# Software pipelining of a transformer layer over 16 sequences: output product and first normalisation of a sequence placed in the next sequence's attention half, its feed-forward one half later

## The reference, cut to what matters

```python
x = _layernorm(x + attention(x))        # 16 heads of 16, window of 128 keys; 4 latent heads; sigmoid gate mixes
x = _layernorm(x + ffn(x))              # ternary weights, 256 -> 1024 -> 256, exact gelu, RMS norm ahead of each
# attention: mixed = gate * local + (1 - gate) * remote;  return mixed @ out_w + out_b
# ffn:       h = gelu(rms(x) @ w_up_q.T);  return rms(h) @ w_down_q.T
```

## Time and profile before

| what | value |
|---|---|
| median of 3 runs | 1309.5 us (1309.12 to 1319.59) |
| profiled execution, its own time | 1306.51 us |
| its span, first to last instruction | 1304.8 us |
| busy: PE, DVE, ACT, POOL | 1071.0, 963.8, 666.2, 686.1 us |
| mean granted clock of TensorE | 0.922 of full speed |
| first exponential of body 0, body 14, body 15 | 120.5, 1161.7, 1229.5 us |

### The profile page before, as it was taken

How to read it: one execution, slowest core, us unless ns; L and a number is a source line. 1 busy time by engine, 2 the same in 40 slices (tenths; PEclk the granted TensorE clock), 3 DMA queues, 4 the chain that set the end, 5 groups by cost and what they waited for, 6 DMA issues and landing times.

```text
span 1304.8 us, 37906 instructions
## 1 busy us (share of the span) xinstructions
PE 1071.0 (82%) x15776; PEld 685.5 (53%) x15776; DVE 963.8 (74%) x2048; ACT 666.2 (51%) x1026; POOL 686.1 (53%) x870
## 2 busy tenths in 40 slices
PE   2566889798988989897998989899888989795855
PEld 1344555464655556464655556465555646464533
DVE  5856768778787887878787877878787887866445
ACT  1213555564646556464646556364655556462624
POOL 6542637373654736364554637265473737364553
PEclk9778989899998999899999989899998989997887
DMA  5845180735537181644628082543719173541000
GB/s 153 139 79 110 43 139 30 125 64 91 92 75 123 37 134 48 115 82 76 107 66 132 30 136 54 106 76 76 122 44 137 46 120 69 98 68 35 2 18 17
DMA packets 57019, 108.08 MB, mean 83 GB/s; under 512 B 14192, under 2 KB 40944, under 8 KB 53744
## 3 DMA queue, kind: packets, MB, share of 16 engines
q1 hardware_dynamic: 56848, 105.66, 44.1%
HBM read 71.55 MB, written 34.08 MB: 81 GB/s over the span
## 4 chain that ended last, share of the span: by engine, by line
PE 52%; DVE 28%; ACT 9%; issue 4%; POOL 4%; SPq 1%; DMA 1%; DVEq 0%; POOLq 0%; ACTq 0%
PE work L1477 9%; PE oacc L1405 7%; PE oacc L1424 6%; PE work L1230 5%; PE work L1348 5%; PE scores L1385 3%; DVE x L1058 3%; PE work L1415 3%; ACT Pt L760 3%; DVE x L1066 3%; DVE nmax L1000 2%; PE scores L1230 2%; DVE ytok L1134 2%; DVE Pt L966 2%; DVE lat_st L963 2%
## 5 line engine op out<-in xcount | busy, mean ns | idle before, releaser
L760 ACT ACTIVATE Pt<-scores 128x1024 f32<-128x1024 f32 (+1 forms) x256 | 228.3, 914 | 115.4 <-PE oacc L1405 83.2
L626 POOL TENSOR_TENSOR h_lo<-hbuf,h_hi 128x512 f16<-128x512 f32 x128 | 148.3, 1159 | 249.6 <-DVE h_hi L1114 249.6
L1000 DVE TENSOR_REDUCE nmax<-work 128x3 f32<-128x480 f32 x352 | 216.5, 636 | 27.8 <-PE work L1353 23.9
L598 POOL TENSOR_SCALAR_AFFINE_SELECT Pt<-Pt 128x512 f32<-128x512 f32 x256 | 163.2, 638 | 109.6 <-ACT Pt L760 108.1
L1477 PE MATMUL work<-xnT,wup_t 128*128 128x512 f16 x512 | 156.6, 444 | 32.5 <-DVE xnT L1102 32.1
L1348 PE MATMUL work<-Ks,Qs 98*32 98x160 bf16 x4096 | 141.5, 237 | 33.0 <-DVE nmax L1000 28.7
L1405 PE MATMUL oacc<-Pt,Vp 128*32 128x256 f32 (+1 forms) x2048 | 149.6, 359 | 3.5 <-POOL Pt L602 3.0
L1255 PE MATMUL scores<-xT,wqk 128*128 128x512 f32 x256 | 116.5, 609 | 19.3 <-ACT xT L695 19.3
L1385 PE MATMUL scores<-Qs,Ks 100*32 100x160 bf16 (+4 forms) x4096 | 113.7, 228 | 13.5 <-ACT Pt L760 10.1
L602 POOL TENSOR_SCALAR_AFFINE_SELECT Pt<-Pt 128x512 f32<-128x512 f32 x192 | 122.0, 635 | 0.0
L1424 PE MATMUL oacc<-wdn_t,h_hi 128*128 128x256 f16 x512 | 120.2, 276 | 0.2
(11 more groups left out here) (169 smaller groups left out, 2088.8 us busy)
## 6 DMA issues: line engine op xcount, KB each, us to landing
parts_scratch<-parts SPq DMA_DIRECT2D x96, 256.0 KB, 6.8
Qs<-parts_scratch SPq DMA_DIRECT2D x96, 256.0 KB, 9.2
Ks<-parts_scratch SPq DMA_DIRECT2D x96, 256.0 KB, 8.9
xtok<-L_attn_x SPq DMA_DIRECT2D x16, 512.0 KB, 13.7
xres<-L_attn_x SPq DMA_DIRECT2D x16, 512.0 KB, 14.8
y<-ytok SPq DMA_DIRECT2D x16, 512.0 KB, 3.2
Qs<-L_ffn_w_up SPq DMA_DIRECT2D x1, 1024.0 KB, 5.6
Qs<-L_ffn_w_down SPq DMA_DIRECT2D x1, 1024.0 KB, 7.6
```

Source lines behind the costliest of these rows:

```text
L598: ins = pool.affine_select(out=pt[:, :, 0:P], in_=pt[:, :, 0:P], compare_op=ALU.is_gt, fill=0.0, base=0, pattern=[[0, 4], [1, P]], channel ...
L626: pool.tensor_tensor(h_lo[:, t % NR, :], hbuf[:, t % 2, :], h_hi[:, t % NR, :], ALU.subtract).then_inc(h_lo_ready, 1)
L760: nc.scalar.activation(Pt[:, u % NPT, :, 0:w], scores[:, slot, :, :].rearrange("p k (h q) -> p (k h) q", h=2)[:, :, 0:w], ACT.Exp, scale=S ...
L1000: nc.vector.tensor_reduce(nmax[:, :, :].rearrange("p b h -> p (b h)")[:, first:first + n], work[:, slot, 0:n * BAND].rearrange("p (h c) -> ...
```

## The change

The change makes a body carry three sequences. The attention half of s now also holds the "early" steps of sequence s-1: transpose of the mix, output product, statistics, normalisation, transpose and split in two float16 parts, spread over the units by a table. The second half holds the feed-forward of s-1, the gate of s (three steps "G") and the projections of s+2. There are 17 bodies; the first has no s-1, the last has only s-1.

Work changes engines: `h_hi` is a second gelu on ACT in place of DVE's cast; the sum of the mix, the product `lat_bd` and the low part of the normalised x go from DVE to POOL (the last by way of a new float32 copy `xnF` that ACT makes). The third and second parts of query and key slices get steps of their own ("R"). The statistics of the last normalisation come at the end of the second half ("L"), its scaling in units 2 to 5 of the body after. `mixed`, `xnF` and a second `ytok` are new buffers.

```diff
+EARLY = {1: [MIX_T], 2: [MIX_T + 1], 4: [OUT], 5: [OUT + 1], 6: [STATS], 8: [NORM], 9: [NORM_X],
+         12: [XN_T], 13: [XN_T + 1], 14: [XN_HI], 15: [XN_HI + 1, XN_LOW], 16: [XN_LOW + 1]}
 SECOND_HALF = (
-    ("P", X_T), ("F", GATE), ("P", QK), ("F", MIX), ("P", QK + 1), ("P", QK + 2), ("P", QK + 3),
-    ("F", MIX_T), ("P", LAT_IN), ("F", OUT), ("P", VALUES), ("P", VALUES + 1), ("P", LAT_SCORES),
-    ("F", NORM), ("P", LAT_SCORES + 1), ("P", VALUES + 2), ("P", VALUES + 3), ("F", XN_T),
-    ("P", LAT_NORM), ("F", UP), ("F", UP + 1), ("P", LAT_T), ("F", UP + 2), ("P", LAT_T + 1),
-    ("F", UP + 3), ("P", LAT_O), ("F", UP + 4), ("P", REMOTE), ("F", UP + 5), ("P", REMOTE + 1),
-    ("F", UP + 6), ("F", UP + 7), ("F", END))
+    ("P", X_T), ("G", GATE_O), ("P", QK), ("F", UP), ("R", 0), ("P", QK + 1), ("F", UP + 1), ("R", 1),
+    ("P", LAT_IN), ("P", QK + 2), ("F", UP + 2), ("R", 2), ("P", QK + 3), ("F", UP + 3), ("R", 3),
+    ("G", GATE_Z), ("P", LAT_SCORES), ("P", LAT_SCORES + 1), ("P", VALUES), ("F", UP + 4), ("G", GATE_MIX),
+    ("P", VALUES + 1), ("F", UP + 5), ("P", VALUES + 2), ("F", UP + 6), ("P", VALUES + 3),
+    ("P", LAT_NORM), ("F", UP + 7), ("P", LAT_T), ("P", LAT_T + 1), ("F", END), ("P", LAT_O),
+    ("P", REMOTE), ("P", REMOTE + 1), ("L", 0))
+def attention_step(u):
+    order = [("S", u + 1)] if u + 1 < NU else []
+    order += [("A", v) for v in A_OF[u][:1]]
+    order += [("E", k) for k in EARLY.get(u, [])]
+    order += [("V", u - 2)] if u >= 2 else []
+    order += [("A", v) for v in A_OF[u][1:]]
+    order += [("O", (u - 7) // NB)] if u >= 7 and (u - 7) % NB == 0 and (u - 7) // NB < HG - 1 else []
+    return order + [("T", t) for t in range(2) if u == T_AT[t]]
...
-            def f_step(s, k):
-                if k == GATE:
+            def gate_step(s, k):
+                if k == GATE_MIX:
 
                     pool.wait_ge(gate_g, count(s, 1, 0))
                     for b in range(NB):
                         rv = rem[:, s.par, b, 0:D].rearrange("p (h d) -> p h d", h=H)
                         pool.tensor_tensor(rv, rv, gate[:, 2, b, :].unsqueeze(2).to_broadcast([P, H, HD]),
                                            ALU.mult).then_inc(rem_part, 1)
+                        pool.wait_ge(rem_part, count(s, NB, b))
+                        pool.wait_ge(mixed_part, count(s, NB, b))
+                        pool.tensor_tensor(mixed[:, b, :], mixed[:, b, :], rem[:, s.par, b, 0:D], ALU.add
+                                           ).then_inc(mixed_ready, 1)
...
-                    gelu = nc.scalar.activation(hbuf[:, t % 2, :], work[:, slot, :], ACT.Gelu)
+                    nc.scalar.activation(hbuf[:, t % 2, :], work[:, slot, :], ACT.Gelu).then_inc(h_act, 1)
+                    if t >= NR:
+                        act.wait_ge(down_done, count(s, FT, t - NR))
+                    nc.scalar.activation(h_hi[:, t % NR, :], work[:, slot, :], ACT.Gelu).then_inc(h_hi_ready, 1)
```

More of the change, by code:

```diff
@@ L164, in work_use @@
 def work_use(s, phase, k):
[L169 to L177, removed]
+    return WORK_USE[phase, s.i, k]
 def p_use(s, result):
-    at = (P_ORDER_FIRST if s.known and s.i < 2 else P_ORDER).index(result)
+    at = (P_ORDER_FIRST if s.i < 2 else P_ORDER).index(result)
     return at % 4, s.i * P_PER[at % 4] + at // 4
@@ L196, in over_sequences @@
 def over_sequences(body):
-    for i in range(B):
-        body(Seq(i, i % 2, i // 2))
+    for i in range(B + 1):
+        body(Seq(i))
 def build(nc, x, qkv_w, qkv_b, rq_w, rq_b, rkv_w, rkv_b, rout_w, rout_b, out_w, out_b, gl_w, gr_w,
@@ L329, in build @@
         oT_ready = sem("oT_ready")
+        g_vec = sem("g_vec")
+        xn_low = sem("xn_low")
         f_vec = sem("f_vec")
@@ L488, in body @@
                     load_x(later)
[L489 to L492, removed]
+                if s.i >= 2:
+                    store(Seq(s.i - 2))
+                if s.exists:
+                    load_xres(s)
+                if s.next().exists:
                     move_max(s.next())
@@ L755, in weights @@
                     act.wait_ge(pv_done, count(s, NU, u - NPT))
-                if u == 1 and not s.last:
+                if u == 1 and s.next().exists:
                     act.wait_ge(part2, count(s.next(), 4, 3))
@@ L811, in body @@
                         copy_o(s, (u - 6) // NB)
-                    if not s.last:
+                    if s.next().exists:
                         for t in range(2):
@@ L1160, in body, with last_norm @@
+            def last_norm(s, b):
+                if b == 0:
+                    dve.wait_ge(rstd2_ready, count(s, 1, 0))
+                y = ytok2[:, s.par, b, :]
+                nc.vector.tensor_scalar(y, y, mv[:, b, 0:1], rs[:, 0, b:b + 1], ALU.subtract, ALU.mult
+                                        ).then_inc(y_ready, 1)
             def body(s):
+                f, later = s.before(), s.second_next()
                 for u in range(FIRST_HALF):
-                    if u >= STAT_AT and not s.first:
-                        finish_before(s, u - STAT_AT)
@@ L1164, in body @@
[L1164 to L1177 removed]
+                    if 0 <= u - LAST_AT < NB and s.i >= 2:
+                        last_norm(Seq(s.i - 2), u - LAST_AT)
@@ L1372, in scores_T @@
                 slot, k = score_use(s, u)
-                if u < 2 and not s.last:
+                if u < 2 and s.next().exists:
                     for bank in (2 * slot, 2 * slot + 1):
```

549 lines of the change are left out of this document (291 added, 258 removed).

## The result

The changed kernel takes 1486.2 us (median of four runs, 1482.7 to 1486.8) against 1309.3 us for the kernel before: 1.135 times as long, interval 1.128 to 1.142. The direction was forecast, the size was not: 1372 us were predicted, with 1412 as the high end. The profiled execution spans 1484.8 us, 114.5 more than the predicted span.

A forecast was written before the change was run, and what follows sets the result against it. PE was to bound the first half, the DMA chain to the key copies to floor the second: 32.4 + 46.6 = 79.0 us per body. 120.5 + 66.3 + 13 x 79.0 + 156.5 = 1370, with 1.7 around it 1372; range 1314 to 1412.

The forecast's parts named there:

- 120.5 + 66.3 + 13 x 79.0 + 156.5 = 1370.3: Whole span: 120.5 us ahead of body 0, 66.3 for body 0, thirteen bodies of 79.0, 156.5 for bodies 14 to 16.
- First half: 26.6 + 5.8: First half of a body: 26.6 us of PE work plus 5.8 of waiting in order between engines, 32.4 together.
- The third rival: Second half: POOL and ACT pass the DMA floor, clock falls another 0.03 (1.5 us); body 83.4, total 1429; chance 0.11.
- the fourth rival: ACT stands as long again after each table load, 1.3 us on the path once per body: 1389; chance 0.05.
- Third part at 12.3: Second half: POOL finishes the third part of the second query slice at 12.3 us (11.5 to 13.5).
- Transfers from there to the landing, 34.0: Second half: DMAs from the end of that third part to the landed key copies take 34.0 us, unchanged.
- Second half 46.6: Second half of a body: 46.6 us (46.4 to 50), first maxima at 46.5, DMA floor 46.3.
- Slices 5 to 7 behind the gate on POOL: Second half: POOL's gate runs to 35.3 us; h_lo of slices 5 to 7 follows at 36.4, 38.4 and 40.3.
- Body 16: Last body: early steps alone 17, eight slices 19.5, end 3.9, last normalisation and store 8; 48.5 us.
- Body 14: Body without projections or DMA chain: first half 32 and second half 25, 57 us together.
- body 15: Body without maxima, projections or DMA chain: first half 26 and second half 25, 51 us together.
- Slower by over 1%: Whole kernel against the one before: the outcome slower had chance 0.82, faster by over 1% 0.06, within 1% 0.12.

The follow-up runs named there:

- x5: Changed kernel with 26 small filling products of PE per body, in unused columns beside the transposed maxima, ahead of maxima group 15: 1432.9 us (1.097).
- x6: x5 with four more groups of filling products, ahead of the first scores and in the second half of the changed kernel: 1410.8 us (1.080).
- x9: Changed kernel with the four sums of the gated mix given back from POOL to VectorE: 1509.6 us (1.157).

## Why the prediction was off

By its own sum, 120.5 + 66.3 + 13 x 79.0 + 156.5 = 1370.3. The trace after has 128.4, 65.8, 1105.7 and 184.9 in those places, so the 114.5 us are +7.9, -0.5, +78.7 and +28.4.

**Bodies 1 to 13, +78.7: the step that failed.** "First half: 26.6 + 5.8" priced PE's work at full clock because the old first half had 1.00, and left it there after adding 5.8 us of waits. The waits came to the sum priced (5.3 measured); the work took 32.5. x5 and x6 show that it is the clock: with fills in the waits and at 1.00 the bodies take 79.6, and 71.4 of the 78.7 us are back. The third rival had the mechanism, but in the second half and for 1.5 us; the second half's clock did fall as it said, from 0.93 to 0.89, but it was the first half that fell far, from 1.00 to 0.82.

The Trainium skill (ScalarE: Activation LUTs, What ACT_TABLE_LOAD costs) adds a drain of about 1380 ns to each load. That was the ground of the fourth rival, and the prediction said that no run could show it. The trace of before could, where the wait for PE behind a load is shorter than such a drain; in the trace of after ACT waits for nobody in this place. Before, then after:

```profile
1138.19 1.28 ACT L796 ACT_TABLE_LOAD   x1
1139.64 0.60 ACT L796 ACTIVATE hbuf<-work 128x512 f32<-128x512 f32 x1 [0.17 <-PE work L1477]
```
```profile
763.20 1.28 ACT L854 ACT_TABLE_LOAD   x1
764.49 0.60 ACT L854 ACTIVATE hbuf<-work 128x512 f32<-128x512 f32 x1
```

The GELU after starts 1.29 us after the load began, 1.28 of them the load itself, and the load begins 0.02 us after the ACTIVATE ahead of it has ended. Before, the GELU came 1.45 us after the load began, 0.17 of them a wait for PE. The measurement decides: 1.28 per load here, and that rival should have had no chance.

**The rest of the body held.** Third part at 12.3: 11.6. Transfers from there to the landing, 34.0: the key copies landed at 44.9 to 47.3 in bodies 1 to 13, so 33.3 to 35.7 us later, 33.9 in the median. Second half 46.6: 47.4. Slices 5 to 7 behind the gate on POOL, h_lo at 36.4, 38.4 and 40.3: the burst ran from 768.63 to 774.60 and the low parts ended at 775.75, 778.53 and 780.33, so at 35.3, 38.0 and 39.8.

**The end, +28.4.** Body 16 was right (48.5; 48.8). Body 14 was put at 57 and took 68.1, body 15 at 51 and took 68.0. Of these 28.1 us, 4.7 are the first half of body 14 (36.7 against 32), the same clock: in x6 it takes 32.5 at 1.00. The first half of body 15 (35.8 against 26) holds 12.1 us of idle time where the 26 left some 4 (old work 16.2 and 5.9 of early steps): without maxima to give between the scores PE waits 5.3 us for an exponential that stands behind ACT's normalised copy (1391.71 to 1393.33), itself late because DVE waited 2.78 us for the root on POOL before it made x1. The two second halves (31.4 and 32.2 against 25) have PE busy 20.5 and 22.1 at 0.89 and 0.81. How their 13.6 us divide between waits and clock, no run settles: no fills stood there.

**Prologue, +7.9: a move that I priced at nothing.** `lat_bd` went from DVE to POOL, and in the first sequence it stands there behind the reduction over partitions of the weight scale. After, POOL and PE:

```profile
47.52 0.40 POOL L664 PARTITION_ALL_REDUCE alpha<-alpha  x1 [8.29 <-issue]
55.36 0.71 POOL L603 TENSOR_TENSOR lat_bd<-rk_sb,diag_mask 128x256 f32<-128x256 f32 x1 [7.44 <-issue]
```
```profile
56.17 2.08 PE L1360 MATMUL scores<-lat_bd,rqT 64*128 64x256 f32 x8 [12.38 <-POOL lat_bd L603]
```

Before, DVE had made it at 43.01, and PE began at 43.95. The 7.44 us in which POOL waits for nothing that the profile shows are not new: before, the first TENSOR_TENSOR on POOL after the same reduction had 7.29 of it, at 81.44, and memsets stood between, the first of them 0.05 us behind the reduction. What POOL does in that time stays open. The move puts a step that PE needs into that place. All experiments on the changed kernel keep this cost. It was read from the trace and not tried by itself.

**The chances.** Slower by over 1% had 0.82, and the range ended at 1412. It had no case in which two halves lose clock together with a late prologue and a late end; the rivals were priced one at a time, and the three large errors had one sign.

## What to carry to other kernels

When steps are moved beside other work, price the work at the clock of a stretch that already has such waits, not at the clock of the stretch that it moves into; where only the clear stretch is at hand, keep the slow price as the range's end. A dependent wait of 3 us in the middle of PE's work cost twice: itself and the slower products behind it. Before sharing an engine's work out, look what stands behind each step in the new engine's queue, in the prologue and the last bodies too, and whether the relieved engine was on the path at all: here its casts weren't.

## What I had not expected of the hardware

In body 7's first half the granted clock fell to 1.2 GHz for 6.9 us at a time, with waits of PE of only 1.8 and 3.2 us ahead, and 26 small products put into the longer one kept it at 2.4 GHz there: 53 us over the whole run, at no cost in the wait. The first TENSOR_TENSOR on GpSimd after a reduction over partitions started 7.3 to 7.4 us late, in both kernels. Fills that had to wait themselves cost 5.5 us a body and gave nothing back. And four sums of 128x256 float32 took 4.29 us on VectorE while GpSimd worked beside it (x9, body 8) and 3.03 on GpSimd, though in the kernel before VectorE needed 0.64 us for one (L1066, mean of 64), which is 2.5 for four.
